# Expert 0's low weight parts made on GpSimd, and the second index list made ahead of the gathers' wait, in a one-core transformer and mixture-of-experts kernel

## The chip, the core and the metric

The kernel runs on one core of one Trainium2 chip. The metric is the device time of one execution in microseconds (us). TensorE is PE in the profile, VectorE is DVE, ScalarE is ACT, GpSimd is POOL and SyncE is SP.

## What is computed

The reference is one block on x of 16 sequences by 256 tokens by 256 features: layer norm plus a shift, 16-head attention with normalised queries and keys, an output projection, and then a mixture of 8 experts in which each expert takes its 512 best tokens of 4096. The last part, which the change touches, is this:

```python
tok = x.reshape(-1, d)
gate = jax.nn.softmax(tok @ Wgate.T, axis=-1)
k_cap = bs // E                                   # 4096 // 8 = 512
vals, idx = jax.lax.top_k(gate.T, k_cap)
...
g = _ln(tok[idx_flat], mlp_g, mlp_b).reshape(k_cap, E, d)
y = jnp.einsum('ked,ehd->keh', g, fc1s) + b1s     # 256 -> 1024
y = jax.nn.gelu(y, approximate=True)
y = jnp.einsum('keh,edh->ked', y, fc2s) + b2s     # 1024 -> 256
y = y * w[..., None]
tok = tok.at[idx_flat].add(y.reshape(-1, d))
```

## The kernel before, in words

Each engine has its own program, and the engines meet at semaphores; the order on an engine is the order in which the code is written. The attention part walks over the 16 sequences in units of two heads (`over_batches`). After it each engine runs its `phase23_...` function once: the routing and the experts.

A product in near-float32 accuracy is made of three fast passes (`three_passes`, L508 to L510): each operand is split into a high part (`_hi`, rounded to the float32r type) and a low part (`_lo`, the full value minus the high part). For an expert the weights come in one transfer into `fcw[par]` (`par` is the expert's number modulo 2); ACT makes `w1_hi` and `w2_hi` (L627, L630), and a subtraction makes `w1_lo` and `w2_lo`.

The routing goes so. The gates are transposed into `gT_`. Then comes the threshold search: 15 steps, each fixing two bits of each expert's threshold. In `search_step` DVE makes trial thresholds from `bits` and `kept` (L840 in the first 7 steps, L843 in the last 8), counts how many gates reach each trial (L845, with an accumulator), shifts `bits` right by two (L847), waits for the totals that PE sums over partitions (L704 or L714), and keeps the best (L849, L850). PE runs filler products (`fill`, L692) between its sums. After the search DVE ranks the chosen tokens (L863 to L888), PE multiplies one-hot matrices into index lists (`list_products`, L742): half 0 holds experts 0 to 3, half 1 experts 4 to 7. For each half, `spread_out(h)` on DVE (L892 to L894) and `spread_lists(pe, h)` on PE (L685) lay the list out over the partitions, and `row_index(h)` on DVE (L899) writes it into `index`.

GpSimd waits for `index` half 0, then issues the gathers of experts 0 and 1, four each (L598), which fetch 128 token rows apiece into `got`. PE transposes expert 0's rows as they land (L755), ACT and DVE scale and split them in two halves of 256 tokens (L661 to L664, L917 to L924), and `expert(0)` starts: first layer for half 0 and half 1 of four column blocks, each block being 128 of the 1024 hidden columns (`hc`), then blocks 4 to 7 for all 512 tokens. ACT applies GELU block by block (L673) into a buffer of two (`yT`), and DVE splits each result (L938, L912). A GELU waits until the block two before it has been split; block 6 on PE waits until GELU 4 has read its PSUM bank.

In the kernel before, DVE makes expert 0's `w1_lo` behind `row_index(0)` (L905), and `row_index(1)` and `w2_lo` (L927) behind the split of the gathered rows. PE's `spread_lists(pe, 1)` stands between the two token halves of expert 0's first layer. SP loads expert 2's weights into `fcw[0]` when `first_w2_lo_ready` has come (L566).

Of the kernel before, what the change touches and what calls it, by code (L numbers as in the profile page):

```python
# [194 lines left out]
def build(nc, x, condT, w_adaT, vecs, w_qk, w_vT, w_outT, w_gateT, experts, b2s, consts, out):  # L195
    ctx = ExitStack()
    with ctx:
# [348 lines left out]
        def raw_w(par):  # L546
            return fcw[par][:, 0:W1], fcw[par][:, W1:W1 + W2]

        def flat(t):
            return t[:, :, :].rearrange("p a n -> p (a n)")  # L550
# [32 lines left out]
        def phase23_pool(pool, refine):  # L583

            refine(B - 1, 4, 1)
            pool.wait_ge(index_ready, 1)
            pool.wait_ge(gates_out, 16)
            pool.wait_ge(row_out, B * 16)
            pool.wait_ge(tok_out, B * 16)

            def gather(e):
                par = e % 2
                if e == 4:
                    pool.wait_ge(index_ready, 2)
                if e >= 2:
                    pool.wait_ge(weights_kept, e - 1)
                for k in range(KT):
                    nc.gpsimd.indirect_dma_start(  # L598
                        out=got[par][:, k, :], out_offset=None, in_=rows_dram,
                        in_offset=bass.IndirectOffsetOnAxis(ap=index[:, e * KT + k:e * KT + k + 1].bitcast(U32), axis=0),  # L600
                        compute_op=ALU.bypass).then_inc(first_gathered[k] if isinstance(e, int) and e == 0 else gathered[par], 16)

            gather(0)
            gather(1)
            for e in range(E):
                if e + 2 < E:
                    gather(e + 2)
                if e >= 1:
                    pool.wait_ge(scattered, 16 * KT * e)
                for k in range(KT):  # L610
                    pool.wait_ge(y_ready, e * KT + k + 1)
                    nc.gpsimd.indirect_dma_start(  # L612
                        out=out.rearrange("b n d -> (b n) d"),
                        out_offset=bass.IndirectOffsetOnAxis(ap=index[:, e * KT + k:e * KT + k + 1].bitcast(U32), axis=0),
                        in_=yout[e % 2][:, k, :], in_offset=None,
                        compute_op=ALU.add).then_inc(scattered, 16)
            pool.wait_ge(scattered, 16 * KT * E)
# [65 lines left out]
        def spread_lists(pe, h):  # L683
            pe.wait_ge(index_a_ready, h + 1)
            nc.tensor.matmul(spread_bank(h), spread_a[:, h, :, :].rearrange("p a b -> p (a b)"), same_tile,  # L685
                             start=True, stop=True).then_inc(lists_spread, 1)

        def fill(products):


            for _ in range(products):
                nc.tensor.matmul(sc[:, 512:1024], filler[:, 0:P], filler[:, :], start=True, stop=True)  # L692

        def phase23_tensor(pe):
# [52 lines left out]
            list_products(1, range(12))  # L747
            spread_lists(pe, 0)
            list_products(1, range(12, TILES)).then_inc(lists_ready, 1)
            fill(16)  # L750
            for h in range(2):
                for k in range(2):
                    pe.wait_ge(first_gathered[2 * h + k], 16)
# [4 lines left out]
            def expert(e, pair, par):  # L758
# [3 lines left out]
                if first:  # L762
                    for h in range(2):
                        half = slice(h * HALF, (h + 1) * HALF)
                        pe.wait_ge(first_lo_ready, h + 1)
                        for hc in range(4):
                            for c in range(DC):
                                cols = slice(hc * P, (hc + 1) * P)
                                ins = three_passes(fc1_bank(e, hc)[:, half], w1_hi[:, c, cols], w1_lo[:, c, cols],
                                                   gT_hi[:, c, half], gT_lo[:, c, half], c == 0, c == DC - 1)  # L770
                            if h == 1:
                                ins.then_inc(fc1_done, 1)
                        if h == 0:
                            spread_lists(pe, 1)
                else:
                    pe.wait_ge(gT_ready, e)
                    pe.wait_ge(gT_lo_ready, e)
# [43 lines left out]
        def phase23_vector(dve, chain, last_rows):  # L821
# [75 lines left out]
            def row_index(h):  # L897
                dve.wait_ge(lists_spread, h + 1)
                V_.tensor_copy(index[:, h * 4 * KT:(h + 1) * 4 * KT], spread_bank(h)).then_inc(index_ready, 1)  # L899

            spread_out(0)
            row_index(0)
            w1, w2 = raw_w(0)
            dve.wait_ge(w1_hi_ready, 1)
            V_.tensor_tensor(flat(w1_lo), w1, flat(w1_hi).bitcast(F32), ALU.subtract).then_inc(first_w1_lo_ready, 1)  # L905
            spread_out(1)


            dve.wait_ge(b2_in, 16)
# [4 lines left out]
            for h in range(2):  # L914
# [7 lines left out]
                V_.tensor_tensor(gT_lo[:, 1, half], gT[:, 1, half], gT_hi[:, 1, half].bitcast(F32), ALU.subtract)  # L922
                dve.wait_ge(first_hi_ready, h + 1)
                V_.tensor_tensor(gT_lo[:, 0, half], gT[:, 0, half], gT_hi[:, 0, half].bitcast(F32), ALU.subtract).then_inc(first_lo_ready, 1)  # L924
            row_index(1)
            dve.wait_ge(w2_hi_ready, 1)
            V_.tensor_tensor(flat(w2_lo[0]), w2, flat(w2_hi[0]).bitcast(F32), ALU.subtract).then_inc(first_w2_lo_ready, 1)  # L927

            def expert(e, pair, par):

# [834 lines left out]
```

## Time and profile before

| | us |
|---|---|
| median of 3 runs | 1151.21 |
| lowest and highest | 1150.68, 1155.15 |
| the profiled execution | 1149.96 |
| its span, first to last instruction | 1148.2 |
| PE, DVE, ACT, POOL busy | 1091.6, 878.9, 728.7, 626.7 |
| mean granted clock of PE | 0.993 of full |

The span is what the rows of the trace add up to; the profiled execution's own time is 1.8 us above it. The last 268 us of the span, from about 880 us on, are routing and experts; the change touches the stretch from 896 to 962 us.

### The profile page before, as it was taken

What the parts mean: (1) busy time and instruction counts of PE and PEld (TensorE: products, weight loads), DVE (VectorE), ACT (ScalarE), POOL (GpSimd) and SP (SyncE); (2) the same over time, 40 slices, a digit from 0 to 9 for tenths busy, and PEclk for the clock granted to TensorE, in tenths of its full rate; (3) what the DMA queues carried; (4) which work ended last, traced back from release to release, by engine and by line L of the source; (5) the groups of instructions that cost most, each with busy time, mean ns of one, the idle gap of its engine ahead of it and who ended that gap; (6) DMA issues with size and microseconds to landing.
All of it is one profiled execution on the core that took longest, in us unless ns stands there. A gap on an engine that the chain in (4) does not pass through costs nothing.

```text
span 1148.2 us, 24631 instructions
## 1 busy us (share of the span) xinstructions
PE 1091.6 (95%) x8046; PEld 859.5 (75%) x8052; DVE 878.9 (77%) x1693; ACT 728.7 (63%) x1991; POOL 626.7 (55%) x656
## 2 busy tenths in 40 slices
PE   8899999999999999999999999999988779999996
PEld 6677778777777777777878777777765248889985
DVE  6888787878777877878787887777776867777773
ACT  5767777777777776777777777777773214555441
POOL 2666666666656566566666665666572033553332
PEclk9999999999999999999999999999999999999998
DMA  5000000000001000000000000000003304554422
GB/s 183 19 11 20 19 20 19 18 18 18 18 18 37 18 18 18 18 18 18 18 18 18 18 18 25 29 9 20 11 19 111 108 25 143 159 133 115 110 29 28
DMA packets 31775, 48.62 MB, mean 42 GB/s; under 512 B 7920, under 2 KB 28528, under 8 KB 30448
## 3 DMA queue, kind: packets, MB, share of 16 engines
q1 hardware_dynamic: 25584, 39.49, 10.6%
q0 software_dynamic: 6144, 8.52, 4.0%
q8 instruction: 28, 0.46, 0.2%
q14 instruction: 19, 0.16, 0.0%
HBM read 35.29 MB, written 12.71 MB: 42 GB/s over the span
## 4 chain that ended last, share of the span: by engine, by line
PE 33%; issue 28%; POOL 26%; DVE 7%; ACT 3%; POOLq 1%; DMA 1%; SPq 0%; DVEq 0%; ACTq 0%
POOL prob L1060 11%; POOL qk_lo L1077 10%; PE ch L508 5%; PE ch L510 5%; PE ch L509 5%; POOL qn L965 3%; PE av L1691 2%; PE sc L1592 2%; PE pq L1645 1%; PE mx L1636 1%; PE sc L508 1%; PE sc L510 1%; PE sc L509 1%; DVE hit L845 1%; DVE probT L1421 1%
## 5 line engine op out<-in xcount | busy, mean ns | idle before, releaser
L1060 POOL TENSOR_TENSOR prob<-prob,inverse 128x512 f32<-128x512 f32 x254 | 260.8, 1048 | 247.8 <-DVE inverse L1400 247.8
L1171 ACT ACTIVATE prob<-sc,m 128x256 f32<-128x256 f32 x512 | 235.8, 475 | 116.7 <-DVE m L1472 113.6
L1472 DVE TENSOR_REDUCE m<-sc 128x4 f32<-128x1024 f32 x127 | 155.4, 1224 | 80.3 <-PE sc L1592 80.1
L1421 DVE COPY probT<-mx 128x1024 f32<-128x1024 f32 (+1 forms) x128 | 155.4, 1214 | 57.2 <-PE mx L1636 56.2
L1077 POOL TENSOR_TENSOR qk_lo<-qkT,qk_hi 128x512 fp32r<-128x512 f32 x128 | 171.8, 1342 | 19.1 <-ACT qk_hi L1153 19.0
L508 PE MATMUL ch<-w_hi,hT_lo 128*128 128x512 f32 x384 | 169.7, 442 | 2.6 <-DVE hT_lo L1333 2.2
L509 PE MATMUL ch<-w_lo,hT_hi 128*128 128x512 f32 x384 | 151.6, 395 | 0.0
L510 PE MATMUL ch<-w_hi,hT_hi 128*128 128x512 f32 x384 | 151.4, 394 | 0.0
L1691 PE MATMUL av<-probT,V 128*64 128x256 f32 x1024 | 138.8, 392 | 6.8 <-DVE probT L1421 2.9
L1636 PE MATMUL mx<-con,prob 128*128 128x128 f32 x1024 | 134.1, 273 | 2.7 <-POOL prob L1060 2.7
L1636 PEld LDWEIGHTS mx<-con,prob 128*128 128x128 f32 x1024 | 117.4, 140 | 16.7 <-POOL prob L1060 3.1
L1691 PEld LDWEIGHTS av<-probT,V 128*64 128x64 f32 x1024 | 62.0, 136 | 66.0 <-DVE probT L1421 30.3
L612 POOL DMA_INDIRECT out<-yout,index x32 | 52.3, 1634 | 101.3 <-DVE yout L958 94.9
L1171 ACT ACTIVATION_READ_ACCUMULATOR prob<-sc,m 128x1 f32 x512 | 105.3, 206 | 0.0
L1361 DVE TENSOR_REDUCE ssum<-sq 128x8 f32<-128x512 f32 x128 | 86.8, 678 | 16.1 <-ACT sq L1128 16.1
L673 ACT ACTIVATE yT<-ch,b_sb 128x512 f32<-128x512 f32 x62 | 42.6, 689 | 88.6 <-PE ch L510 78.2
L1126 ACT ACTIVATE raw<-ch 128x512 f32<-128x512 f32 x128 | 78.8, 615 | 30.0 <-PE ch L510 30.0
L508 PEld LDWEIGHTS ch<-w_hi,hT_lo 128*128 128x128 f32 x384 | 72.1, 188 | 26.6 <-issue 1.9
L1592 PE MATMUL sc<-qk_hi,qk_lo 64*128 64x256 f32 x512 | 85.5, 330 | 2.5 <-ACT prob L1171 2.0
L1645 PE MATMUL pq<-con,qn 128*128 128x128 f32 x512 | 77.6, 274 | 10.0 <-POOL qn L965 7.3
L1592 PEld LDWEIGHTS sc<-qk_hi,qk_lo 64*128 64x128 f32 x512 | 48.2, 184 | 50.7 <-issue 47.9
L1187 ACT ACTIVATE qkT<-pq,q_vec 128x256 f32<-128x256 f32 x128 | 73.8, 577 | 18.4 <-PE pq L1645 18.4
(222 smaller groups left out, 2656.3 us busy)
## 6 DMA issues: line engine op xcount, KB each, us to landing
fcw<-experts SPq DMA_DIRECT2D x8, 2048.0 KB
x_sb<-x SPq DMA_DIRECT2D x16, 256.0 KB, 2.7
xr_sb<-x SPq DMA_DIRECT2D x16, 256.0 KB, 2.7
out<-tok SPq DMA_DIRECT2D x16, 256.0 KB, 2.2
rows_dram<-xh SPq DMA_DIRECT2D x16, 256.0 KB, 2.2
prob<-w_qk SPq DMA_DIRECT2D x2, 512.0 KB, 6.7
qn<-w_qk SPq DMA_DIRECT2D x2, 512.0 KB, 7.0
V<-w_vT SPq DMA_DIRECT2D x2, 512.0 KB, 6.8
```

The costliest lines, as they stand in the source:

```text
L508: nc.tensor.matmul(psum, l_lo, r_hi, start=first, stop=False)
L509: nc.tensor.matmul(psum, l_hi, r_lo, start=False, stop=False)
L510: return nc.tensor.matmul(psum, l_hi, r_hi, start=False, stop=last)
L1060: nc.gpsimd.tensor_tensor(pr, pr, r, ALU.mult).then_inc(normalised, 1)
L1077: nc.gpsimd.tensor_tensor(qk_lo[par][:, :], qkT[par][:, :], qk_hi[par][:, :].bitcast(F32), ALU.subtract).then_inc(lo_ready, 1)
L1171: ins = nc.scalar.activation(prob[hp % 2][:, g * N:(g + 1) * N], sc[:, g * N:(g + 1) * N], ACT.Exp, bias=m[hp % 2][:, g:g + 1], scale=-1.0 ...
L1421: nc.vector.tensor_copy(probT[:, 0:half], mx[:, 0:half]).then_inc(probT_ready, 1)
L1472: nc.vector.tensor_reduce(m[hp % 2][:, :], sc[:, :].rearrange("p (g n) -> p g n", n=N), AX.X, ALU.min).then_inc(max_ready, 1)
L1592: ins = nc.tensor.matmul(sc[:, at:at + N], q_part[par][rows, it * P:(it + 1) * P], k_part[par][rows, N:2 * N], start=(q_part is qk_lo), st ...
L1636: ins = nc.tensor.transpose(mx[:, to:to + P], pr[:, at:at + P], ident)
L1645: ins = nc.tensor.transpose(pq[:, at * P:(at + 1) * P], qn[gpar][:, c, i * P:(i + 1) * P], ident)
L1691: ins = nc.tensor.matmul(av[hh * HD:(hh + 1) * HD, 0:N], V[gpar][:, jt, i * P + hh * HD:i * P + (hh + 1) * HD], probT[:, at:at + N], start ...
```

## The change

GpSimd makes expert 0's two low weight parts, as soon as ACT has made the high parts, which is during the threshold search. DVE no longer makes them. DVE makes the second index directly behind the first. PE lays the second list out after 6 of the 16 filler products that stand ahead of the first rows' transposes, not between the two halves of the first layer, and it waits for that index before the transposes.

```diff
@@ phase23_pool
             refine(B - 1, 4, 1)
+            w1, w2 = raw_w(0)
+            pool.wait_ge(w1_hi_ready, 1)
+            nc.gpsimd.tensor_tensor(flat(w1_lo), w1, flat(w1_hi).bitcast(F32), ALU.subtract).then_inc(first_w1_lo_ready, 1)
+            pool.wait_ge(w2_hi_ready, 1)
+            nc.gpsimd.tensor_tensor(flat(w2_lo[0]), w2, flat(w2_hi[0]).bitcast(F32), ALU.subtract).then_inc(first_w2_lo_ready, 1)
             pool.wait_ge(index_ready, 1)
@@ phase23_tensor
-            fill(16)
+            fill(6)
+            spread_lists(pe, 1)
+            fill(10)
+            pe.wait_ge(index_ready, 2)
...
-                        if h == 0:
-                            spread_lists(pe, 1)
@@ phase23_vector
-            spread_out(0)
-            row_index(0)
-            w1, w2 = raw_w(0)
-            dve.wait_ge(w1_hi_ready, 1)
-            V_.tensor_tensor(flat(w1_lo), w1, flat(w1_hi).bitcast(F32), ALU.subtract).then_inc(first_w1_lo_ready, 1)
-            spread_out(1)
+            for h in range(2):
+                spread_out(h)
+                row_index(h)
...
-            row_index(1)
-            dve.wait_ge(w2_hi_ready, 1)
-            V_.tensor_tensor(flat(w2_lo[0]), w2, flat(w2_hi[0]).bitcast(F32), ALU.subtract).then_inc(first_w2_lo_ready, 1)
```

The program of GpSimd between its last small step of the attention part and the gathers; before:

```order
L1020 TENSOR_TENSOR na<-na,var 128x36
L1022 TENSOR_TENSOR na<-three_halves,na 128x36
L1028 TENSOR_TENSOR rstd<-na,guess 128x36
L598 DMA got<-rows_dram,index 128x264 x12
L612 DMA out<-yout,index 4096x256 x4
```

And of the changed kernel (its lines after the insertion are 5 or 6 higher):

```order
L1028 TENSOR_TENSOR rstd<-na,guess 128x36
L588 TENSOR_TENSOR w_lo<-fcw,w_hi 128x2048
L590 TENSOR_TENSOR w_lo<-fcw,w_hi 128x2048
L603 DMA got<-rows_dram,index 128x264 x12
L617 DMA out<-yout,index 4096x256 x4
```

Two subtractions of 128 x 2048 now stand ahead of the first gather.

The program of DVE from the first index list to the first split of gathered rows; before:

```order
L899 CAST index<-pq 128x16
L905 TENSOR_TENSOR w_lo<-fcw,w_hi 128x2048
L892 COPY parts<-ch 128x16
L893 SCALAR_TENSOR_TENSOR index_a<-parts,ch 128x16
L894 TENSOR_TENSOR spread_a<-index_a,con 128x128
L917 TENSOR_SCALAR gT<-sc,vec 128x256
```

And of the changed kernel:

```order
L905 CAST index<-pq 128x16
L898 COPY parts<-ch 128x16
L899 SCALAR_TENSOR_TENSOR index_a<-parts,ch 128x16
L900 TENSOR_TENSOR spread_a<-index_a,con 128x128
L905 CAST index<-sc 128x16
L920 TENSOR_SCALAR gT<-sc,vec 128x256
```

The subtraction is gone from between the two lists, and the second index cast has come up to it. In the kernel before, that cast and the second subtraction stood ahead of the first split of a GELU result on DVE:

```order
L924 TENSOR_TENSOR gT_lo<-gT,gT_hi 128x256
L899 CAST index<-sc 128x16
L927 TENSOR_TENSOR w_lo<-fcw,w_hi 128x2048
L935 COPY row_w<-got 128x4
L938 CAST yT_hi<-yT 128x512
```

The changed kernel has neither there; `row_w` and the first `yT_hi` follow the rows' split directly.

## Rows read from the trace of the kernel before

**Rows 1.** The page: the span.

```profile
span 1148.2 us, 24631 instructions
```

**Rows 2.** Timeline, DVE in the search: start us, duration us, instruction, idle before.

```profile
898.52 0.48 DVE L845 TENSOR_SCALAR_CACHE_REDUCE hit<-gates_T,trial 128x256 bf16<-128x256 f32 x1
...
898.92 0.17 DVE L847 TENSOR_SCALAR bits<-bits 128x4 int32<-128x4 int32 x1
...
899.87 0.16 DVE L843 TENSOR_TENSOR trial<-bits,kept 128x3 int32<-128x3 int32 x1
...
902.02 0.16 DVE L843 TENSOR_TENSOR trial<-bits,kept 128x3 int32<-128x3 int32 x1
```

**Rows 3.** Timeline, DVE from the first index to the first GELU split.

```profile
936.11 3.39 DVE L905 TENSOR_TENSOR w_lo<-fcw,w_hi 128x2048 fp32r<-128x2048 f32 x1
...
950.93 0.18 DVE L899 CAST index<-sc 128x16 int32<-128x16 f32 x1 [2.63 <-PE sc L685]
951.02 2.28 DVE L927 TENSOR_TENSOR w_lo<-fcw,w_hi 128x2048 fp32r<-128x2048 f32 x1
...
953.29 0.42 DVE L938 CAST yT_hi<-yT 128x512 fp32r<-128x512 f32 x1
```

**Rows 4.** Timeline, ACT: high parts, then GELUs of expert 0.

```profile
898.22 1.89 ACT L630 ACTIVATE w_hi<-fcw 128x2048 fp32r<-128x2048 f32 x1
...
951.07 1.26 ACT L673 ACTIVATE yT<-ch,b_sb 128x512 f32<-128x512 f32 x2 [3.42 <-PE ch L510]
```

**Rows 5.** Timeline, PE: first and last transposes of gathered rows, expert 0's first layer.

```profile
942.71 0.38 PE L755 MATMUL sc<-con,got 128*128 128x128 f32 x2
...
946.16 0.33 PE L755 MATMUL av<-con,got 128*128 128x128 f32 x1 [0.84 <-DMA got<-rows_dram,index]
...
949.25 0.29 PE L685 MATMUL sc<-con,spread_a 128*128 128x16 f32 x2
949.39 0.37 PE L508 MATMUL ch<-gT_hi,w_lo 128*128 128x256 f32 x1
...
952.28 0.40 PE L508 MATMUL ch<-gT_hi,w_lo 128*128 128x512 f32 x1
...
954.85 0.40 PE L510 MATMUL ch<-gT_hi,w_hi 128*128 128x512 f32 x1
957.73 0.80 PE L508 MATMUL ch<-gT_hi,w_lo 128*128 128x512 f32 x1 [2.48 <-ACT yT L673]
...
962.04 1.04 PE L789 MATMUL mx<-con,got 128*128 128x128 f32 x8
```

**Rows 6.** Timeline, GpSimd around the first gathers.

```profile
936.48 4.04 POOL L598 DMA_INDIRECT got<-rows_dram,index  x1 [55.20 <-DVE index L899]
940.83 0.98 POOL L598 DMA_INDIRECT got<-rows_dram,index  x1 [0.30 <-issue]
```

**Rows 7.** Timeline, GpSimd: two subtractions of 128 x 1024 in the attention part.

```profile
14.35 4.78 POOL L1039 TENSOR_TENSOR w_lo<-V,w_hi 128x1024 fp32r<-128x1024 f32 x2 [7.55 <-ACT w_hi L1114]
```

**Rows 8.** One line, L1077: min/median/max ns of 128 x 512.

```profile
L1077 POOL TENSOR_TENSOR qk_lo<-qkT,qk_hi x128: 1274/1289/1737, 30.0 to 862.9; 128x512 fp32r<-128x512 f32 x128
```

**Rows 9.** Timeline, GpSimd and DVE side by side at 100 us.

```profile
99.97 1.22 POOL L965 TENSOR_TENSOR qn<-raw,rstd 128x512 f32<-128x512 f32 x1
...
100.33 1.41 DVE L1333 TENSOR_TENSOR hT_lo<-hT,hT_hi 128x512 fp32r<-128x512 f32 x1
```

**Rows 10.** Timeline, GpSimd and DVE side by side at 857 us.

```profile
856.75 1.04 POOL L1060 TENSOR_TENSOR prob<-prob,inverse 128x512 f32<-128x512 f32 x1
...
857.15 0.66 DVE L1374 TENSOR_SCALAR var<-mv 128x4 f32<-128x4 f32 x1
```

**Rows 11.** Windows: us, busy time of each engine, granted PE clock, DMA share.

```profile
903.00:908.30 5.30, 3.34 (x16) 1.14 (x15) 4.23 (x25) 0.00 (x0) 0.00 (x0) 1.00 0.68 69
957.90:960.50 2.60, 2.60 (x7) 2.02 (x8) 2.45 (x5) 0.69 (x1) 0.49 (x1) 0.50 0.89 354
```

**Rows 12.** Timeline, PE: one sum in the search with the wait before it.

```profile
908.34 0.18 PE L704 MATMUL av<-cnt,same_b 128*128 128x3 bf16 x1 [1.34 <-DVE hit L845]
```

## The prediction, made before the changed kernel was run

> **What bounds the kernel now.** I read the page first, then the windows to find the stage, then the timelines of DVE, ACT, GpSimd and PE side by side, since a change of a few us is decided by single instructions. The span is 1148.2 us [rows 1]; the change works inside 65 us of it. Two stretches matter. In the search DVE is the bound. A step of the later kind runs from one L843 to the next, 899.87 to 902.02, so 2.15 us, and inside it DVE hardly waits [rows 2]. The work is tiny instructions of 0.16 to 0.48 us, each needing the one before, so whatever holds one of them up holds up everything behind: ranking, lists, gathers, experts. GpSimd does nothing there; it has been idle 55.20 us when its first gather starts [rows 6]. The second stretch is expert 0's first layer. PE computes blocks 4 and 5 from 952.28 on, stops behind 954.85, and stands 2.48 us until ACT's GELU 4 has emptied a bank [rows 5]. GELU 4 is late because DVE splits the first GELU only at 953.29, though the first two GELUs ran from 951.07 to 952.33: DVE was busy with the second index (950.93) and with `w2_lo`, 2.28 us [rows 3, 4]. After its stop PE also goes on at half clock, 0.50 granted from 957.90 to 960.50, the lower of its two levels (1.2 against 2.4 GHz), whereas a wait of 1.34 us at 908.34 lies in a stretch granted 1.00 [rows 11, 12].
>
> **Part 1, what leaves DVE and PE.** (a) The layout product of list 1 leaves the first layer. It puts the next pass from 949.25 to 949.39, so 0.14 us is won; where it goes, among the fillers, it lengthens a queue that waits for gathered rows anyway (the last transposes start at 946.16 after a wait of 0.84) [rows 5]. (b) The first two GELUs then start at 950.93 and the first is done 0.69 later (half of the 1.26 for two, plus their overlap) [rows 4]. DVE is free and splits it at 951.65, not 953.29: 1.64 earlier [rows 3]. The chain split, GELU, split keeps its pace, so GELU 4 and PE's block 6 come 1.64 earlier too, 956.09 for 957.73 [rows 5]. (c) PE's stop shrinks from 2.48 to about 1.1, since blocks 4 and 5 end 0.14 earlier. That is under the 1.34 behind which the clock stayed, so I let it stay [rows 5, 11, 12]. Blocks 6 and 7 are 12 passes. At full clock the spacing is (954.85 - 952.28) / 11 = 0.234, so 2.8 us; now they take 962.04 - 957.73 = 4.31 [rows 5]. That is 1.5 more. Together the layer ends 1.64 + 1.51 = 3.15 us earlier. If the clock falls in spite of the shorter stop, only 1.6 is left. From there PE runs through the second layer and the following experts, so the end moves with it. SP's load of expert 2's weights also starts earlier, when `w2_lo` is done; it waits for nothing else and nobody waits for it there, so I cost it at nothing.
>
> (d) `w1_lo` leaves the place beside the first gather. That gather took 4.04 us against 0.98 for the second, and the subtraction beside it 3.39 against 2.28 for the same form at 951.02. The subtraction ended at 939.50 and the gather 1.02 later [rows 3, 6]. If the gather had waited for DVE, it would now shrink to about 1 us. But PE has its 16 fillers in front and reaches the first transpose at 942.71, without waiting; four pairs of transposes behind that end about 944.3 at best, against 946.16 now [rows 5]. So this is worth 0 to 1.9. A first call that is long by itself gives 0. I take 0: the cover is uncertain, and the split of the rows on DVE still lies behind. The Trainium skill speaks to it (SBUF — State Buffer, Who interferes with whom): a two-tensor instruction takes only the read side of the port pair that VectorE shares with GpSimd, and descriptor generation needs the write side, which the page calls inferred. By that the gather did not wait for the subtraction and the term is 0; by the rows' ends it could be up to 1.9.
>
> **Part 2, what GpSimd now does, and what it costs DVE.** The size: two subtractions of 128 x 1024 take 4.78, so 2.39 each [rows 7]; one of 128 x 512 takes 1.29 [rows 8]. The difference, 1.10 per 512 columns, gives 2.39 + 2.20 = 4.6 for 128 x 2048. ACT starts the second high part at 898.22 [rows 4], so the first is ready at 898.3. GpSimd works from about 898.4 to 903.0 and, its second input ready at 900.1, from 903.0 to 907.6. By itself that costs nothing: its gathers come at 936.
>
> But DVE and GpSimd get in each other's way. At 99.97 GpSimd runs a multiplication until 101.19. DVE starts a subtraction with two SBUF inputs at 100.33, and it is reported as 1.41 us, ending at 101.74, after GpSimd [rows 9]. A plainer case is at 857.15: a DVE TENSOR_SCALAR of 4 columns, SBUF to SBUF, takes 0.66 us, where one of 4 columns in the search takes 0.17 [rows 2, 10]. It ends at 857.81, and the GpSimd instruction beside it at 857.79. So the small one stood still until about 0.15 before GpSimd was through. It was not slowed in proportion. In the search two of DVE's instructions have such forms: L847 (TENSOR_SCALAR, SBUF to SBUF, 4 columns) and L843 (TENSOR_TENSOR, both inputs in SBUF) [rows 2]. With 4.6 us on the other side this is no trifle:
> - L847 starts at 898.92 and stands until 903.0 - 0.15 = 902.85; it is done at 903.0.
> - L849, L850 and L843 follow at some 0.2 each, so L843 starts at 903.5. GpSimd has begun its second subtraction at 903.0. L843 stands until 907.6 - 0.15 = 907.45 and is done at 907.6, for 900.03 before.
> - The search is 7.6 us late. All else in it, and all behind it, keeps its pace.
>
> The bound below is 0, if these forms do not meet GpSimd because they are integer; the one above takes in L845, below. PE has no sums to do meanwhile and stops for some 7 us, so its clock will be low for a few us after. Its six fillers and a sum then nearly fill a step of 2.15; I allow 0 to 0.5.
>
> The Trainium skill (same page and section) says it as a rule: a VectorE instruction in a two-port mode, or with two SBUF inputs against a GpSimd instruction that reads, is shut out for the whole of the other's instruction, and the form that also writes its accumulator has no two-port mode. By the rule L845 goes through and the sum is the 7.6 above; by sharing in proportion it would be far less. The two rows have the whole-instruction picture; that L845 is spared no row shows, as GpSimd is idle whenever it runs.
>
> **The sum.** +7.6 - 3.15 = +4.45. Against the profiled execution, 1149.96, that is 1154.4; against the median of the runs, 1151.21, it is 1155.7. The profiled execution lies 1.25 below the median and 0.7 below the fastest run. I forecast 1155.0.
>
> **Rivals.**
> - *Only the two-input form is shut out.* L847's kind stands in the trace for float32 only; here it is an integer shift. Then L843 stands from 899.87 to 902.85 and is done at 903.0, 3.0 late; the next one, due at 905.0, meets the second subtraction and is done at 907.6, for 902.18 before. That is 5.4 late; with 3.15 off, +2.25: 1152.2 to 1153.5. Chance 0.20.
> - *The other side: nothing in the search is shut out*, since all is integer or of a few columns. For it: no row has an integer instruction beside GpSimd. Against it: the 4 columns at 857.15 were held [rows 10]. Then -3.15, or -5.0 with the gather's 1.9: 1145 to 1148, likeliest 1147.5. It decides from the point where DVE loses less than 3.15 us in the search. Chance 0.12.
> - *L845 is shut out as well.* It is the third of its step, starts at 898.52 [rows 2], stands until 902.85, and L847 behind it meets the second subtraction: done at 907.6 or a little later, for 899.09. That is 8.5 to 8.9 late: +5.5 to +5.9, 1155.4 to 1157.1. Chance 0.10.
> - *The blocked search plus a clock that is low at a bad place* (the search's steps stretched by 0.5, block 6 and 7 still at half clock, 1.5): +6.0 to +6.5, 1156 to 1158. Chance 0.08.
>
> **How the numbers follow.** My forecast has 0.50; with gather 0 shorter it falls to +2.6, with slow steps it rises to +5.0, so its own range is 1152.6 to 1156.5. The range 1148.0 to 1158.0 leaves out most of the unblocked case and little above. About 0.5%, 5.8 us, is what a measurement of this kernel can tell from no change. The forecast and the first rival lie within it; the unblocked case too, but for its far end; L845 blocked lies at its edge, and the clock case beyond it. Faster 0.03, same 0.83, slower 0.14.
>
> **What would show it.** In the changed kernel's trace: GpSimd's two subtractions at about 4.6 us each from 898.4; L847's successor with one duration near 4 us; one L843 successor near 4 us (two of about 3 and 2.5, and no long shift, for the first rival); the first gather's start about 7.6 later than 936.48; its duration near 4 again; the first GELU's split right behind the GELU; PE's stop at block 6 about 1.1 and the clock 1.00 behind it. I am wrong if the short instructions keep their 0.16 us, if DVE keeps the turn between its L847 and L843, or if the second subtraction is late enough to let a whole step through.

## The result, and the profile after

The changed kernel takes 1166.51 us (median of 4 runs, 1164.61 to 1168.87), the kernel before 1150.95 on the same chip (4 runs, 1150.58 to 1155.15): ratio 1.0132, 95% interval 1.0117 to 1.0147. It is slower, 15.6 us by the medians, and outside the range I gave. The profiled executions took 1166.61 and 1149.96; their spans differ by 16.5 us.

The page of the changed kernel has

```profile
span 1164.7 us, 24632 instructions
```

In the search, GpSimd's timeline (as in [rows 6]: start, duration, instruction, idle before) is

```profile
901.61 4.51 POOL L588 TENSOR_TENSOR w_lo<-fcw,w_hi 128x2048 fp32r<-128x2048 f32 x1 [18.17 <-ACT w_hi L632]
906.08 4.50 POOL L590 TENSOR_TENSOR w_lo<-fcw,w_hi 128x2048 fp32r<-128x2048 f32 x1
```

and DVE's beside it:

```profile
901.74 0.48 DVE L851 TENSOR_SCALAR_CACHE_REDUCE hit<-gates_T,trial 128x256 bf16<-128x256 f32 x1
...
902.13 4.01 DVE L853 TENSOR_SCALAR bits<-bits 128x4 int32<-128x4 int32 x1
906.28 0.16 DVE L855 SCALAR_TENSOR_TENSOR kept<-av,trial 128x3 f32<-128x3 f32 x1
906.75 0.16 DVE L856 TENSOR_REDUCE kept<-kept 128x1 f32<-128x4 f32 x1 [0.30 <-DVE kept L855]
906.94 3.65 DVE L849 TENSOR_TENSOR trial<-bits,kept 128x3 int32<-128x3 int32 x1
```

The reader sees the two holds of the prediction: the shift, 0.17 in [rows 2], stands until GpSimd's first subtraction is nearly over, and the trial, 0.16 before, until the second is. L851 (L845 of before) starts while GpSimd runs and keeps its 0.48.

What was not predicted is at the gathers. GpSimd's first gather, 4.04 in [rows 6], now takes 1.15:

```profile
946.99 1.15 POOL L603 DMA_INDIRECT got<-rows_dram,index  x1 [36.42 <-DVE index L905]
948.44 0.97 POOL L603 DMA_INDIRECT got<-rows_dram,index  x1 [0.30 <-issue]
```

It and seven more run to 956.96, each 0.30 behind the other. PE meanwhile is in the last 80 products of list 1:

```profile
946.42 1.72 PE L747 MATMUL ch<-val_b,one_a 128*32 128x32 bf16 x52
948.30 0.45 PE L747 MATMUL ch<-val_b,one_a 128*32 128x32 bf16 x6 [0.16 <-issue]
949.05 0.44 PE L747 MATMUL ch<-val_b,one_a 128*32 128x32 bf16 x6 [0.31 <-issue]
...
952.79 0.29 PE L747 MATMUL ch<-val_b,one_a 128*32 128x32 bf16 x2 [1.11 <-issue]
...
959.45 0.61 PE L690 MATMUL sc<-con,spread_a 128*128 128x16 f32 x2 [3.38 <-DVE spread_a L900]
...
966.97 0.36 PE L508 MATMUL ch<-gT_hi,w_lo 128*128 128x256 f32 x1 [1.49 <-DVE gT_lo L927]
...
978.58 1.04 PE L795 MATMUL mx<-con,got 128*128 128x128 f32 x8
```

The first 52 products take 1.72 us, the other 28 another 4.9, in handfuls with pauses in which PE waits for nothing that the profile shows. DVE, which waits for the last of them, goes on much later still:

```profile
946.53 0.17 DVE L905 CAST index<-pq 128x16 int32<-128x16 f32 x1 [0.50 <-PE pq L690]
958.69 0.17 DVE L898 COPY parts<-ch 128x16 f32<-128x16 f32 x1 [11.99 <-remote]
...
971.55 0.43 DVE L938 CAST yT_hi<-yT 128x512 fp32r<-128x512 f32 x1 [3.07 <-ACT yT L678]
```

PE ended its last product at 953.08, 5.6 us before DVE saw it. The wait ends 0.4 behind the eighth gather's rows (in the DMA view of 956 to 960 us the last packets lie at 958.2 to 958.3); the profile names no engine as its releaser ("remote"). In expert 0's first layer all is as predicted or better: the first GELU (970.84 for two) is split at 971.55, and PE has no wait between 966.97 and 978.58. The windows (us, busy time of each engine, PE clock, DMA share, GB/s) show the clock low behind the holds and in the stall, and full in the layer:

```profile
908.30:928.00 19.70, 12.65 (x49) 4.62 (x51) 16.17 (x78) 0.00 (x0) 2.27 (x1) 0.78 0.34 114
946.00:959.00 13.00, 7.04 (x93) 4.45 (x89) 0.48 (x4) 0.00 (x0) 7.84 (x8) 0.70 0.31 84
966.90:978.00 11.10, 11.00 (x70) 9.74 (x71) 7.75 (x17) 4.80 (x8) 3.88 (x4) 1.00 0.18 50
```

To set the two kernels side by side I take four marks. Of before, the timeline of all engines has

```profile
880.97 0.42 DVE L826 TENSOR_REDUCE top<-logit 128x32 f32<-128x256 f32 x1
...
936.02 0.17 DVE L899 CAST index<-pq 128x16 int32<-128x16 f32 x1 [0.53 <-PE pq L685]
...
946.35 0.36 PE L508 MATMUL ch<-gT_hi,w_lo 128*128 128x256 f32 x1
```

These are the start of routing (nothing ahead of it is changed), index 0, and the start of the first layer; the fourth is the transposes of expert 1's rows behind that layer, 962.04 in [rows 5]. Start of routing is 883.13 in after. The differences:

| stretch | before | after | change |
|---|---|---|---|
| to the start of routing (code unchanged) | 880.97 | 883.13 | +2.2 |
| routing to index 0 | 55.05 | 63.40 | +8.35 |
| index 0 to first layer | 10.33 | 20.44 | +10.1 |
| first layer to next transposes | 15.69 | 11.61 | -4.1 |

Their sum is the 16.5. The first row is a draw: over the eighteen profiles of this study it lies between 880.69 and 883.49 in kernels that are all alike up to there. The second row holds another: the first trial of the search comes 3.65 behind the start of routing in before and 4.70 in after, though GpSimd's subtractions start 14 us later; in the other profiles it lies between 3.65 and 5.75, and at 4.69 in `w1_before_lists`, which is the kernel before up to there. So the change itself costs 13.3 to 14.4 in the profile, somewhat less than the 15.6 of the medians.

### The profile page after: what moved, and what is told of

It reads as the page before. It is cut to its first block, busy times and chain, and to the rows that moved or that the text cites. A ratio compares the mean times of both kernels' runs of the same rounds, so it can differ in the third digit from the quotient of the medians.

```text
span 1164.7 us, 24632 instructions
## 1 busy us (share of the span) xinstructions
PE 1098.7 (94%) x8046; PEld 862.3 (74%) x8052; DVE 880.4 (76%) x1691; ACT 728.1 (63%) x1991; POOL 632.3 (54%) x658
## 4 chain that ended last, share of the span: by engine, by line
PE 34%; issue 28%; POOL 25%; DVE 7%; ACT 3%; another core or an unknown queue 1%; POOLq 1%; DMA 0%; SPq 0%; DVEq 0%; ACTq 0%
POOL prob L1060 11%; POOL qk_lo L1077 9%; PE ch L508 5%; PE ch L510 5%; PE ch L509 5%; POOL qn L965 3%; PE av L1691 2%; PE sc L1592 2%; PE sc L697 1%; PE pq L1645 1%; PE mx L1636 1%; PE sc L508 1%; PE sc L509 1%; PE sc L510 1%; DVE hit L851 1%
## 5 line engine op out<-in xcount | busy, mean ns | idle before, releaser
L1077 POOL TENSOR_TENSOR qk_lo<-qkT,qk_hi 128x512 fp32r<-128x512 f32 x128 | 171.8, 1342 | 21.2 <-ACT qk_hi L1153 21.0
L510 PEld LDWEIGHTS ch<-w_hi,hT_hi 128*128 128x128 f32 x384 | 72.3, 188 | 17.8
```

The costliest lines, as they stand in the source:

```text
L510: return nc.tensor.matmul(psum, l_hi, r_hi, start=False, stop=last)
L1077: nc.gpsimd.tensor_tensor(qk_lo[par][:, :], qkT[par][:, :], qk_hi[par][:, :].bitcast(F32), ALU.subtract).then_inc(lo_ready, 1)
```

## The experiments

The table gives the same marks of every kernel from its profile (us; "list 2" is the time from index 0 to VectorE's work on list 1, which stands second; "first layer" runs to the next transposes), and the ratio to before. The first column holds the draw ahead of the first trial, up to 2.1.

| kernel | routing to index 0 | index 0 to list 2 | index 0 to first layer | first layer | ratio, 95% |
|---|---|---|---|---|---|
| before | 55.05 | 3.4 | 10.33 | 15.69 | |
| after | 63.40 | 12.2 | 20.44 | 11.61 | 1.0132 [1.0117, 1.0147] |
| w1_before_lists | 55.36 | 12.1 | 14.50 | 12.92 | 1.0028 [1.0014, 1.0042] |
| pool_only | 62.96 | 12.1 | 15.36 | 12.08 | 1.0074 [1.0056, 1.0092] |
| lists_first | 65.32 | 0.1 | 7.42 | 18.58 | 1.0089 [1.0072, 1.0107] |
| shifted_fetch | 64.64 | 12.1 | 20.51 | 11.59 | 1.0124 [1.0107, 1.0141] |
| index_only | 54.14 | 4.1 | 11.06 | 12.27 | 0.9982 [0.9972, 0.9991] |
| w2_between_halves | 55.37 | 4.3 | 11.24 | 12.83 | 0.9979 [0.9970, 0.9988] |
| gathers_apart | 65.18 | 6.5 | 15.02 | 11.59 | 1.0091 [1.0075, 1.0106] |
| w1_beside_gather | 58.72 | 2.9 | 14.63 | 13.86 | 1.0070 [1.0054, 1.0085] |
| late_weights | 59.43 | 3.6 | 10.68 | 19.14 | 1.0048 [1.0033, 1.0064] |
| paced_gathers | 65.29 | 0.1 | 7.41 | 15.74 | 1.0056 [1.0038, 1.0074] |
| update_behind_wait | 62.84 | 12.0 | 20.24 | 11.57 | 1.0130 [1.0114, 1.0145] |
| low_part_in_list_wait | 58.42 | 0.1 | 7.61 | 14.17 | 0.9981 [0.9970, 0.9991] |
| update_then_stop | 63.00 | 12.0 | 20.12 | 11.60 | 1.0127 [1.0106, 1.0147] |
| load_ahead | 63.68 | 11.9 | 20.34 | 11.58 | 1.0130 [1.0114, 1.0146] |
| landing_paced | 64.06 | 2.9 | 13.66 | 17.01 | 1.0103 [1.0085, 1.0121] |
| half_and_half | 54.03 | 2.4 | 9.62 | 12.97 | 0.9974 [0.9964, 0.9985] |

**Where the stall comes from.** Theory A: gathers that follow each other hold back what PE sends, and in the kernel before `w1_lo` on DVE kept the first gather from starting that flow before list 1 was through. Rival B: the subtractions on GpSimd bring it. `w1_before_lists` is the kernel before with one statement moved:

```
+            w1, w2 = raw_w(0)
+            dve.wait_ge(w1_hi_ready, 1)
+            V_.tensor_tensor(flat(w1_lo), w1, flat(w1_hi).bitcast(F32), ALU.subtract).then_inc(first_w1_lo_ready, 1)
             spread_out(0)
             row_index(0)
-            w1, w2 = raw_w(0)
-            dve.wait_ge(w1_hi_ready, 1)
-            V_.tensor_tensor(flat(w1_lo), w1, flat(w1_hi).bitcast(F32), ALU.subtract).then_inc(first_w1_lo_ready, 1)
             spread_out(1)
```

> Kernel before, with one edit: DVE makes w1_lo in its wait for the lists (it stands idle 4.1 us there), not beside the first gather. GpSimd gets no subtraction, the index code is as before. Theory A (the gathers, once nothing on DVE holds the first one back, run beside PE's last list products, and PE and the update that tells DVE of list 1 come late): the first gather takes about 1.15 us for 4.04, DVE's second list starts only when the gathers have landed (about 6 us or more late), and the kernel is 5 to 10 us slower than before. Theory B (the stall in the changed kernel comes from the two subtractions on GpSimd): no stall, time as before or up to 1 us less.

It measured 1154.04 (1151.15 to 1156.02) against 1151.02. Its GpSimd starts with

```profile
938.95 1.15 POOL L598 DMA_INDIRECT got<-rows_dram,index  x1 [55.51 <-DVE index L899]
```

and its DVE has

```profile
950.56 0.17 DVE L892 COPY parts<-ch 128x16 f32<-128x16 f32 x1 [11.90 <-remote]
```

The gather is short and the 12 us are there, with nothing else on GpSimd: B falls. The price, 3 us, is smaller than the 5 to 10 that A had named: 4.2 us between index 0 and the first layer, less 2.8 in the layer. `pool_only`, the kernel before with GpSimd's part of the change alone, sorts the two halves of the change:

> Kernel before, with only the move of w1_lo and w2_lo to GpSimd; index code as before. The search is 7.5 us late (one shift held about 4.0, one trial held about 3.65) by every theory. Theory A: first gather 1.15 us, and DVE's second list held until the gathers land, so the split of the gathered rows is held too: total +13 to +17 over before. If the stall needs the new index code instead: +3 to +5.

It measured 1160.42 (1158.22 to 1162.11), 9.4 above before on its chip, between the two expectations: 7.9 in the search, 5.0 between index 0 and the first layer, -3.6 in the layer. The 5.0 are PE's: its last product ends 6.6 behind index 0 (2.2 in before), the fillers behind it run at a clock of 0.61, and PE reaches the first transposes 12.5 behind index 0 (6.7 in before). DVE, held until 957.64, is free again when these are through. The other 5.1 of after's 10.1 come from the new order of TensorE: the transposes stand behind list 1's layout and ten fillers, so they start only after the held update is through.

**What the hold asks for.** `lists_first` is after with PE making all products of list 1 ahead of list 0's layout:

```
-            list_products(1, range(12))
+            list_products(1, range(TILES)).then_inc(lists_ready, 1)
             spread_lists(pe, 0)
-            list_products(1, range(12, TILES)).then_inc(lists_ready, 1)
```

> Changed kernel, with PE doing all 256 list products before it lays out list 0, so that no gather can run beside a list product. Theory A: the stall of DVE's second list (12.0 us, of which about 10 is lost) is gone, index 0 comes 2 us later, so 7 to 9 us less than the changed kernel. Theory C (the stall is of the gathers with whatever PE does, its fillers too): the update of the second layout comes late instead and less than 4 us is won.

It measured 1161.56 (1160.00 to 1163.87), 5 below after, less than A's 7 to 9. The products no longer falter and the first layer comes 13 us sooner behind index 0. But now twelve gathers run without a pause from 948.05 to 963.07, and ACT's first GELU is held:

```profile
965.24 1.26 ACT L678 ACTIVATE yT<-ch,b_sb 128x512 f32<-128x512 f32 x2 [8.93 <-remote]
```

PE had ended that GELU's bank at 958.8, and the last gather's rows were there at 964.4. The hold has moved from list 1 to the layer, which makes A wider: not only the list products, but PE's updates.

`gathers_apart` is after with `pool.wait_ge(index_ready, 2)` between `gather(0)` and `gather(1)`:

> The changed kernel, but GpSimd starts expert 1's four gathers only when index 1 is written; the first four go as before. Theory A (held as long as gathers follow each other): VectorE's wait for list 1 ends when the fourth gather lands, 6 to 7.5 us behind index 0 in place of 12.0, and 4 to 6 us of the time come back: 1160.5 to 1163. Rival F (the hold is a fixed time, or what TensorE itself does with its products): the wait still ends about 12 us behind index 0, and the time stays at 1165 to 1168 or grows, as expert 1's rows come later.

1161.49 (1160.35 to 1162.96). DVE's wait ended 6.5 us behind index 0, in A's range:

```profile
954.54 0.17 DVE L899 COPY parts<-ch 128x16 f32<-128x16 f32 x1 [6.35 <-PE ch L748]
```

It ended with PE's last product (954.5), 1.1 us after the fourth gather was issued and 0.2 ahead of its last rows (954.7 to 954.8). So this update was not held at all, not even until the fourth gather had landed, as A had it; what made it late is the faltering products. `landing_paced` goes further, each gather waiting for the rows of the one before:

```
                 for k in range(KT):
+                    if isinstance(e, int) and (e == 0 and k > 0 or e == 1 and k == 0):
+                        pool.wait_ge(first_gathered[(k - 1) % KT], 16)
```

> The changed kernel, but each of the first four gathers starts only when the one before has landed, and expert 1's when the fourth has. Theory A as it stands (it takes gathers that follow each other without a pause): the last products of list 1 run without pauses, VectorE's wait for list 1 ends 3 to 5 us behind index 0. If one gather under way is enough: products and update are late still, by 1 to 4 us. In both the rows come late: a gather takes some 2.7 us to land, so the fourth lands 11 us behind index 0 in place of 6.5; time 1160 to 1166, no test of the theory by itself.

1163.26 (1160.51 to 1165.51). PE's 80 products ran through, and DVE waited 2.69 for them:

```profile
946.77 2.93 PE L749 MATMUL ch<-val_b,one_a 128*32 128x32 bf16 x80
```

One gather under way does nothing; several behind each other do.

Four kernels looked for the way in which they do it. `shifted_fetch` puts 60 products of 8 columns more on PE ahead of the lists, `load_ahead` 90 (and 4 fillers fewer), so that a load of PE's instructions does not meet the gathers:

> Changed kernel, with 60 tiny products (8 columns) on PE in its wait for val_b, where it stands idle 1.07 us. They put 120 instructions ahead of the lists, so that PE's instruction load of 16384 bytes (at 948.04 in the changed kernel, inside the first gather) falls before the first gather. Theory D (PE starves because that load falls into the gathers' traffic): the list products run through and the kernel is 8 to 11 us faster than the changed one, less up to 1 us for the tiny products. Theory A: stall as in the changed kernel, time within 2 us of it.

> The changed kernel with 90 products of 8 columns more on TensorE in its wait for the part values, and 4 fillers fewer: the program stands 86 products further on when list 1 comes. The profile's DMA view has a load of 16 KB of instructions 1.05 us behind the start of the first gather in the changed kernel; here it should start 1.0 us ahead of it and be over when the gathers start. Theory D (a load of TensorE's instructions that meets the gathers starves it and holds its updates): the last products of list 1 run without pauses, VectorE's wait ends 3 to 5 us behind index 0, time 1157 to 1162. Theory A (the gathers hold what TensorE sends, wherever the loads stand): wait 11.5 to 12.2 us, 1164.5 to 1168.

1166.21 (1164.32 to 1167.48) and 1165.81 (1164.53 to 1166.81). In `load_ahead` the DMA view from 945.4 to 947.1, ahead of the first gather at 947.12, has

```profile
q8 instruction: 1, 0.02, 4.9%
```

and from 947.1 to 950.2 none (in `shifted_fetch` the load lies at 946.8, 0.5 ahead of the first gather). Faltering and hold are unchanged (11.74): a load that meets the gathers is not the cause. `update_then_stop` drops the six fillers behind the update, `update_behind_wait` gives the update on a filler product that waited for the fourth gather's rows:

```
-            list_products(1, range(12, TILES)).then_inc(lists_ready, 1)
-            fill(6)
+            list_products(1, range(12, TILES))
+            pe.wait_ge(first_gathered[3], 16)
+            nc.tensor.matmul(sc[:, 512:1024], filler[:, 0:P], filler[:, :], ...).then_inc(lists_ready, 1)
+            fill(5)
```

> The changed kernel without the six filler products that TensorE runs right behind its last product of list 1, so that TensorE stands still as soon as it has given the update. If updates come through the gathers' flow when TensorE stops behind them (as those of the row transposes do): VectorE's wait for list 1 ends 6.5 to 7.5 us behind index 0 in place of 12.0, time 1160.5 to 1163. If the update is held whatever TensorE does: the wait still ends 11.5 to 12.2 us behind index 0, 1164.5 to 1168.

> The changed kernel; the update that says list 1 is ready is given not by TensorE's last list product but by a filler product behind it, ahead of which TensorE waits for the fourth gather's rows (they land about 6.5 us behind index 0, when the products have just ended). Gathers 5 to 8 still follow without a pause. Theory A1 (any update of TensorE is held while gathers follow each other): VectorE's wait for list 1 still ends 11.5 to 12.2 us behind index 0, time 1165 to 1168. Theory A2 (only the updates of TensorE's products that ran on without a wait are held; one given behind a wait comes through): it ends 7 to 8 us behind index 0, and about 4 us of the time come back, 1161.5 to 1164.

1164.89 (1163.05 to 1167.42) and 1166.51 (1163.69 to 1166.83), with waits of 11.82 and 11.77. What PE does around the update does not matter, in these two forms. Yet other updates come through in such a flow. Those behind the row transposes do: ACT's answer to the second pair in the kernel before comes at 946.63, right behind PE's last transpose (946.32, 0.27 long), with gathers from 940.83 to 949.38. So do some of the first layer: in `w2_between_halves` (gathers from 951.66 on, 0.30 apart) and `paced_gathers` (from 955.47 on) the first GELU starts 0.10 behind its bank's last product, as it does in after. These came in the second and third gather of a run. Those that were held came in the fourth or later, but so did some that passed. What decides is open.

**The rest of the sum.** `index_only` is before with TensorE's and VectorE's half of the change:

> The kernel before with the index half of the change alone: list 1's layout product right behind list 1 on TensorE, its index right behind its layout on VectorE. Both low parts stay on VectorE where they were, so the first low part still lies beside the first gather. Theory A (TensorE's updates are held back while gathers follow each other without a pause, and the first low part used to hold the first gather until the lists were through): nothing is held, VectorE's second list starts within 4 us of index 0, the first GELU's split still waits for the second low part; within 1 us of before, ratio 0.999 to 1.001. Rival: the new index order is itself a cost, since after lies 6 us above pool_only; then this kernel is 3 to 6 us above before.

1148.66 (1146.47 to 1151.12) against 1151.51. It is a little faster, not the same: the second low part no longer waits for index 1 and starts at 949.15, the first GELU is split at 951.86, PE's stop is 0.72 for 2.48, the layer takes 12.27 for 15.69. So the order alone brings nearly all that I had put down to the move of `w2_lo`; so does that move alone (`pool_only`, 12.08). Either half is enough, and they do not add. In `w2_between_halves` DVE takes `w2_lo` between the two halves of the rows:

> index_only, and VectorE takes the second low part between the splits of the two halves of the first rows; nothing runs on GpSimd but the gathers. Theory A: no stall (VectorE's second list within 4 us of index 0), search as before, first split straight behind the first GELU, TensorE without its stop of 2.48 us in the first layer: 3 to 4 us below before, 1147 to 1148. Rival: the gain of the first layer seen in after (4.1 us less from its start to the next transposes) was only the catching up of what the stall had delayed; then within 1 us of before. A second rival: the subtraction of 2.28 us, now beside gathers 2 or 3, holds the rows of the second half back and TensorE stops in the first layer instead; then 1 to 3 us above before.

1149.66 (1146.16 to 1150.37), no better than `index_only`. Its sixth gather took 3.06 beside the 2.28 of `w2_lo`, and PE waited 0.48 for the second half: the second rival's mechanism, at a small size.

`w1_beside_gather` is after with `w1_lo` back on DVE beside the first gather, the second low part still on GpSimd:

> The changed kernel, but the first low part is VectorE's again, beside the first gather; the second low part stays on GpSimd in the search, and the new index order stays. SyncE waits for both. Theory A: the first gather lasts 3 to 4 us again, no stall (VectorE's second list within 4 us of index 0); one subtraction in place of two in the search costs 3.7 to 4.7; the first layer gives 3 to 4 back; 0 to 3 us above before, 1150 to 1154. Rival B (the subtractions on GpSimd bring the stall, by what they leave behind): half or all of it stays, 1157 to 1161.

1158.40 (1158.20 to 1159.67). The gather took 3.56, list 2 came 2.9 behind index 0, and index 0 came 3.7 later: as A says. The time lies in rival B's range all the same, for another reason: the rows were late. SyncE had started to fetch expert 2's weights at 944.5, as my edit made it wait for both low parts, and the window beside the gathers has

```profile
945.00:952.00 7.00, 2.60 (x13) 1.12 (x12) 0.39 (x2) 0.00 (x0) 5.42 (x6) 0.93 0.86 308
```

308 GB/s, a DMA share of 0.86, and PE waiting 4.80 for rows. `late_weights` holds that fetch until the first GELU:

> w1_beside_gather (one low part on GpSimd in the search, the first low part beside the first gather), with SyncE's fetch of expert 2's weights held until the first GELU. In w1_beside_gather it started at 944.5 us and moved 2 MB beside the gathers, and TensorE waited 4.80 us for the first rows. If that transfer was what held the rows: this wait falls under 1 us, the clock stays full in the first layer, and the time falls by 4 to 6.5, to 1152 to 1154.5. Rival: the rows were late because of the gathers themselves, or of GpSimd's subtraction ahead of them: the time stays within 1 us of 1158.4.

1157.55 (1156.52 to 1160.79). In the same window:

```profile
945.00:952.00 7.00, 4.84 (x30) 2.14 (x26) 3.01 (x7) 0.82 (x2) 5.78 (x5) 1.00 0.21 58
```

PE found the first rows there, and none of its three waits for the others was above 0.89, so the transfer had held them. The time stayed in the rival's range, since earlier rows let expert 2's gathers follow without a pause (to 961.52), and the hold caught the first layer: ACT waited 8.50 for its first GELU, to 963.49, though PE had ended its bank at 958.8. I had not expected that, but it is `lists_first` again.

`paced_gathers` takes the stall out of after, with `lists_first`'s order and GpSimd waiting before expert 1's gathers for the row transposes, and before expert 2's for the second GELU:

> The changed kernel (both subtractions on GpSimd in the search, new index order), with all of TensorE's list products ahead of list 0's layout, expert 1's gathers only behind the transposes of expert 0's rows, and expert 2's only behind the second GELU. The stall of the gathers is thus taken away and the rest of the change is left. If the sum on record was right but for that stall (search 7.6, first layer -3 to -4, about 1 for the longer wait to list 0): 1154.5 to 1157.5. Rival: the subtractions on GpSimd cost more than the search shows, or pacing brings a wait of its own (rows of expert 1 late at their transposes): 1159 or more.

1158.41 (1156.59 to 1159.71), 8 below after, ratio 1.0056. It misses the expected 1154.5 to 1157.5 by 1: index 0 is late by 10.2 (8.35 in after, and some 2 for the 80 products that now stand ahead), 2.9 come back to the first layer, and nothing in the layer, where PE stops 2.64 once more: eight gathers run beside it, and ACT's fifth GELU, for which PE waits, has a "remote" wait of 1.48 that ends with the last of them. So the sum on record, without the stall, is about right in the search and too hopeful in this kernel's layer.

`low_part_in_list_wait` and `half_and_half` look for the faster kernel, both from `index_only`. The first makes `w1_lo` in DVE's wait for list 0, with all products ahead of the layout:

> No subtraction on GpSimd. VectorE makes the first low part in its wait for list 0 (3.6 to 4.1 us idle in all runs), TensorE makes all list products ahead of list 0's layout, so that none is left when the gathers start; index 1 early, second low part behind the rows' split. Theory A: nothing of TensorE is left to be held, the first gather lasts 1.15 us, the first transposes come 1 to 2.5 us earlier than in index_only, and with its gains the kernel lies 3 to 5 us below before (1146 to 1148.5). Rival: as in lists_first, the gathers that now run without any pause hold the first layer's updates back, and ScalarE's first GELU comes late by 2 to 8 us: 1151 to 1157.

1149.26 (1146.84 to 1151.70) against 1151.67, between the two expectations and no better than `index_only`: the first layer comes 3.4 us sooner behind index 0, but index 0 is 4.3 later. `w1_lo` took 5.14 there, beside the list products, where it takes 2.28 in the layer. The second splits it:

```
+            V_.tensor_tensor(flat(w1_lo)[:, 0:1024], w1[:, 0:1024], ...subtract)
             spread_out(0)
             row_index(0)
+            V_.tensor_tensor(flat(w1_lo)[:, 1024:], w1[:, 1024:], ...subtract).then_inc(first_w1_lo_ready, 1)
             spread_out(1)
             row_index(1)
```

> index_only with the first low part in two halves: the first in VectorE's idle time ahead of list 0, the second beside the first gather. Nothing on GpSimd. Theory A: the first gather is held for 2.3 to 3 us in place of 4.7, long enough for TensorE's 80 products (2.0 us) to end before the flow slows them; no stall; rows, and the first layer, 1.5 to 2.5 us earlier than in index_only: 1146 to 1147.5. Rival: the hold is too short, TensorE's last products meet the second gather and their update is held to the eighth's landing: 1150 to 1156.

1147.08 (1145.31 to 1149.90) against 1151.04, ratio 0.9974 [0.9964, 0.9985]: 3 to 4 us below before and the lowest ratio of the study, though the intervals of all four kernels below 1 overlap. The first gather took 3.09 and PE's products ran through:

```profile
934.61 2.45 PE L742 MATMUL ch<-val_b,one_a 128*32 128x32 bf16 x80
```

## Why the prediction was wrong

- *The search (Part 2, +7.6).* Right, by mechanism and size. L847's and L843's successors took 4.01 and 3.65, so 3.84 and 3.49 more, 7.3 in all, for 3.91 and 3.66 taken; the subtractions took 4.51 and 4.50 for 4.6. They began 3.2 later than forecast (901.61), by the two draws, 2.2 and 1.05. L845's form kept its 0.48 beside GpSimd, which no row had shown, and L855, with one input in PSUM, and L856 kept their 0.16. From routing to index 0 the change is 8.35: the 7.3, the 1.05 of the first trial, and 0.8 in the steps behind the holds at a low clock (0.78 from 908.3 to 928.0), where I had allowed up to 0.5, less 0.85 that the list products took less. These rows agree with the Trainium skill's rule (SBUF — State Buffer, Who interferes with whom).
- *The first layer (Part 1 a to c, -3.15).* Right in kind; it measured -4.1, as PE's stop did not shrink to 1.1 (0.98 by the sum's own figures: 2.48 - 1.64 + 0.14) but went. The cause was not the move of `w2_lo` alone: `index_only` gets 3.4 with `w2_lo` still on DVE, `pool_only` 3.6 with the old order. And what went beyond the forecast has a cause of its own, below.
- *The first gather (Part 1 d, taken as 0, bounds 0 and a gain of 1.9).* This is the step that failed. `w1_lo` did hold the first gather (4.04 with it, 1.15 without; 3.09 with half of it), and I asked only what an earlier gather could bring. I did not ask what it would meet: the eighty list products on PE and their update. Nor was a loss among the bounds. It cost 10.1: 5.0 by PE's faltering products and the slow fillers behind them (`pool_only`) and 5.1 because the new order puts the transposes behind the held update. The cover that I named for (d), 16 fillers in front of the transposes, was no cover, since what came late stood ahead of them. The Trainium skill's inference, same page and section, that a two-tensor instruction leaves descriptor generation alone, is not borne out: each of the eight gathers that started while DVE was at a low part lasted until 0.8 to 1.0 us behind the end of that subtraction (six first gathers, 3.1 to 4.9 against 1.15, and two later ones, 2.97 in `index_only` and 3.06 in `w2_between_halves`, against 0.96). Two that started ahead of the subtraction, by 0.09 and 0.16, went through (1.00 in `low_part_in_list_wait`, 1.07 in `half_and_half`).
- *The rivals.* None had this. The two-input rival and the unblocked one fall with the two holds seen, the L845 rival with its 0.48. The clock rival holds for the search, not for the layer. The L845 rival's sum is 0.15 too high: 8.5 to 8.9 less 3.15 is 5.4 to 5.8.
- *The draws.* Routing started 2.2 later in after's profile than in before's, and the first trial 1.05 later behind it. That is in no term; in the runs' medians it averages out in part.

The hold was in the kernel before already, and in the prediction's rows. PE ended list 1's layout product by 949.54 [rows 5], and DVE took up the second index, with 2.63 of idle time before it, only at 950.93 [rows 3]. The last product for the first GELU is

```profile
950.06 0.28 PE L510 MATMUL ch<-gT_hi,w_hi 128*128 128x256 f32 x1
```

and the GELU starts at 951.07 [rows 4]. So the two updates arrived 1.4 and 0.7 late; in after the same gaps are 0.05 and 0.10. The DMA view of 949 to 951 has the last packets of the eighth gather at 950.7. I read both waits as waits for PE's work. The layer of after starts when the first eight gathers are through, so its first GELU is not held, and that is 0.6 of the 0.9 that the layer gained beyond the forecast.

With the stall added to the sum (7.6 - 3.15 + 10.1) the forecast would have been 1165.

What is shown: products falter and updates are held while gathers follow each other 0.30 apart; this needs no work on GpSimd but the gathers, moves with them, and goes when the first one is held back or each waits for the rows of the one before (with a pause behind the fourth the update is no longer held, but the products falter still). What stays open: the path on which gathers, PE's instruction flow and its updates meet, and which updates pass.

## What to carry to other kernels

An instruction that runs long beside another engine's may be what keeps that engine in step; before moving it away, ask what the freed engine will start and what is under way then, and give the term a loss as well as a gain. Where a long run of gathers from GpSimd would start while TensorE still has an update that others wait for, try what a little work that holds the first one back does, or pacing. Ask of each wait in a profile whether the work that it is put down to had long ended: here that would have shown the hold beforehand. And take one part of a change alone before costing the whole: here the reordering alone was 2 to 3 us faster than before.

## What the runs showed that I had not expected

- Eight gathers behind each other made PE's bf16 list products falter (28 products in 4.9 us for 0.7) and held its update for 5.6 us after the product, until the eighth had landed. With twelve the first layer's update was held 6.5 us (958.76 to 965.24).
- A fetch of 2 MB at 308 GB/s beside the gathers made PE wait 4.80 us at once for rows; without it no wait was above 0.89.
- DVE's subtraction of 128 x 2048 took 2.28 in the layer, also beside a gather there (`index_only`, `w2_between_halves`), and 2.9 to 4.3 beside the first gather, where PE's list products run too. Beside list products with GpSimd idle it took 3.75 (`w1_before_lists`) and 5.14 (`low_part_in_list_wait`). So the stretch comes where PE's list products run, with or without a gather, and the 3.39 beside the first gather in before need be no sign of the two waiting for each other. No run separates the products out, and why it stretches is open.
- Profiles of kernels alike up to routing differ there by up to 2.8 us (880.69 to 883.49), half of what 0.5% is. A span should be compared stretch by stretch.
